# Batch tiles of 256, 256, 512, 512 and 512 rows with sums of four double steps, paired transposes, field sums on VectorE and paced gathers

## The reference

```python
e = jnp.stack([tbl_f[ids[:, f]] for f in range(32)], axis=1)        # (2048, 32, 64)
z = jnp.sum(e, axis=-1)                                             # field sums, 32 columns
outer = jnp.einsum('bpd,pde,bpe->bp', e[:, II, :], kernels, e[:, JJ, :])   # 496 pairs
h = jnp.concatenate([z, outer, dense_ctx], axis=1)                  # 32 + 496 + 16 = 544
h = jnp.maximum(h @ W_top1 + b_top1, 0.0)                           # 512
h = jnp.maximum(h @ W_top2 + b_top2, 0.0)                           # 256
y = h @ W_top3                                                      # 1
```

## Time and profile before

| | |
|---|---|
| median of three executions | 942.61 us |
| time of the profiled execution | 942.61 us |
| its span | 940.8 us |
| PE busy, matmul instructions | 889.5 us (95%), 4592 |
| DVE busy, instructions | 588.2 us (63%), 500 |
| ACT busy, instructions | 139.7 us (15%), 209 |
| POOL busy, instructions | 484.0 us (51%), 518 |
| mean granted TensorE clock | 0.996 of full speed |

### The profile page before, as it was taken

How to read it: one execution, slowest core, us unless ns; L and a number is a source line. 1 busy time by engine, 2 the same in 40 slices (tenths; PEclk the granted TensorE clock), 3 DMA queues, 4 the chain that set the end, 5 groups by cost and what they waited for, 6 DMA issues and landing times.

```text
span 940.8 us, 11425 instructions
## 1 busy us (share of the span) xinstructions
PE 889.5 (95%) x4592; PEld 280.6 (30%) x4592; DVE 588.2 (63%) x500; ACT 139.7 (15%) x209; POOL 484.0 (51%) x518
## 2 busy tenths in 40 slices
PE   0389999999999999999999999999999999999997
PEld 0122222332333323232333333323333333222232
DVE  0146777777655577767764477767775457777850
ACT  0020202012122020020020311002021212002001
POOL 6777777777777777777775346656630000000000
PEclk9989999999999999999999999999999999999999
DMA  9411111111211111121111001111100000000000
GB/s 334 148 26 27 28 27 27 27 27 27 47 28 27 27 27 27 27 47 27 27 27 21 15 14 23 24 38 23 23 16 1 1 0 1 1 2 20 1 1 0
DMA packets 21018, 29.60 MB, mean 31 GB/s; under 512 B 9188, under 2 KB 9316, under 8 KB 20840
## 3 DMA queue, kind: packets, MB, share of 16 engines
q0 software_dynamic: 16384, 16.81, 9.2%
q1 hardware_dynamic: 4576, 12.07, 3.5%
q10 hardware_dynamic: 8, 0.01, 0.0%
HBM read 27.79 MB, written 1.06 MB: 31 GB/s over the span
## 4 chain that ended last, share of the span: by engine, by line
PE 73%; POOL 19%; issue 6%; DMA 1%; ACT 0%; DVE 0%; DVEq 0%; ACTq 0%
PE y L505 39%; PE acc L519 20%; POOL rows L282 19%; PE y L548 6%; PE y L563 3%; PE spin L491 3%; PE spin L530 1%; PE y L553 1%; PE y L572 1%; DMA rows<-tbl,ids_sb 0%; DMA ids_sb<-ids 0%; ACT h L388 0%; DVE prod L462 0%; DVEq L198 0%; ACT h L400 0%
## 5 line engine op out<-in xcount | busy, mean ns | idle before, releaser
L462 DVE TENSOR_TENSOR prod<-y,xt 128x1024 f32<-128x1024 f32 x496 | 587.6, 1220 | 319.5 <-PE y L505 319.5
L282 POOL DMA_INDIRECT rows<-tbl,ids_sb x512 | 483.3, 944 | 210.4 <-issue 151.2
L505 PE MATMUL y<-xt,kw 64*128 64x512 f32 x1984 | 506.5, 624 | 4.7 <-ACT xt L337 4.7
L519 PE MATMUL acc<-prod,ones_strip 128*32 128x512 f32 x1984 | 265.9, 608 | 0.6 <-DVE prod L462 0.6
L505 PEld LDWEIGHTS y<-xt,kw 64*128 64x128 f32 x1984 | 170.1, 187 | 300.7 <-issue 294.0
L337 ACT COPY xt<-spin 128x512 f32<-128x512 f32 x64 | 37.5, 585 | 500.2 <-PE spin L491 500.2
L519 PEld LDWEIGHTS acc<-prod,ones_strip 128*32 128x32 f32 x1984 | 39.1, 108 | 190.2 <-issue 166.0
L491 PE MATMUL spin<-ident,rows 128*128 128x128 f32 x256 | 43.8, 296 | 40.4 <-DMA rows<-tbl,ids_sb 40.4
L548 PE MATMUL y<-h_in,w_sb 128*128 128x512 f32 x128 | 57.1, 599 | 0.7 <-ACT h_in L366 0.7
L491 PEld LDWEIGHTS spin<-ident,rows 128*128 128x128 f32 x256 | 28.0, 145 | 91.4 <-issue 63.9
L548 PEld LDWEIGHTS y<-h_in,w_sb 128*128 128x128 f32 x128 | 23.7, 190 | 34.2 <-issue 32.6
(11 more groups left out here) (19 smaller groups left out, 41.8 us busy)
## 6 DMA issues: line engine op xcount, KB each, us to landing
rows<-tbl,ids_sb POOLq DMA_INDIRECT x512, 2.4
kw<-pair_k SPq DMA_DIRECT2D x14, 512.0 KB, 11.4
w_sb<-w SPq DMA_DIRECT2D x1, 1024.0 KB, 12.8
sums<-z_sums SPq DMA_DIRECT2D x4, 256.0 KB, 2.5
w_sb<-w SPq DMA_DIRECT2D x1, 512.0 KB, 13.7
z_in<-sums SPq DMA_DIRECT2D x8, 64.0 KB
kw<-pair_k SPq DMA_DIRECT2D x1, 384.0 KB, 17.7
ids_sb<-ids SPq DMA_DIRECT2D x1, 256.0 KB, 2.8
```

What stands on the lines that cost most here:

```text
L282: pool.indirect_dma_start(out=rows[:, s, c, h, :], out_offset=None, in_=tables[f], in_offset=bass.IndirectOffsetOnAxis(ap=ids_sb[:, t, c * ...
L462: nc.vector.tensor_tensor(prod[:, n % PROD_SLOTS, :, :], y_banks[u % Y_SLOTS][:, :, :], x, ALU.mult).then_inc(y_read, 1)
L505: last = nc.tensor.matmul(y[:, h, :], kw[part, d, :], xt[part, slot_of(t, units[h][0] // 2), :], start=True, stop=True)
L519: last = nc.tensor.matmul(acc[32 * q:32 * q + 32, :], ones_strip[:, 30 - 2 * s:62 - 2 * s], prod[:, (N_STEPS * t + u // 2) % PROD_SLOTS, u ...
```

## The change

The tiles have 256, 256, 512, 512 and 512 rows now. A group has four double steps (`GROUP = 4`), and there are eight buffers of `prod`. From the second tile on, couples are transposed in pairs, and they go into a `y` buffer instead of `spin`; ACT copies both at once. The bank that is free holds a second `acc`. DVE forms the field sums from the gathered rows, and PE transposes them (two or four transposes for each tile) in place of the 32 sums. The way through DRAM is gone; SP now loads the dense columns into the same rows. POOL's gathers of the first tile have a memset of 128x256 ahead of each, and every later gather waits for a number of finished products, 32 steps ahead of the transpose and one gather for each step (one for every two steps in a narrow tile).

```diff
-TILES = BATCH // TILE
+WIDTHS = [256, 256, 512, 512, 512]
+TILES = len(WIDTHS)
-GROUP = 2
+GROUP = 4
...
-    for j in range(AHEAD):
-        work[N_STEPS - 5 * (AHEAD - j)].append(("transpose", 1, j))
+    work[N_STEPS - GROUP * (AHEAD // 2 + 1)].append(("fields", 0, 0))
+    for j in range(0, AHEAD, 2):
+        work[N_STEPS - GROUP * (AHEAD - j) // 2].append(("couples", 1, j))
...
-    for j in range(COUPLES):
+    for j in range(0, COUPLES, 2):
         n = COUPLES * t + AHEAD + j
         if n < COUPLES * TILES:
-            work[j * N_STEPS // COUPLES + 2].append(("transpose", *divmod(n, COUPLES)))
+            work[j * N_STEPS // COUPLES // GROUP * GROUP + GROUP].append(("couples", *divmod(n, COUPLES)))
     for d, what in zip(MLP_STEPS, (("mlp1", t - 1, 0), ("mlp1", t - 1, 1), ("mlp2", t - 1, 0), ("mlp3", t - 1, 0))):
-        work[d + GROUP].append(what)
+        work[d].append(what)
...
+    work[56].append(("fields", t, 0))
...
+GATHER_LEAD = 32
+def steps_before_gather(t, k, i):
+    what = Y_ORDER[copy_use(t, k)]
+    count = 2 * rowsets(t)
+    return STEPS_BEFORE[what] - GATHER_LEAD + (i + count * (k - what[2])) * 2 * TILE // P // count
...
-                        pool.wait_ge(spin_full, spin_use("transpose", *divmod(n - GATHER_SLOTS, COUPLES)) + 1)
+                        pool.wait_ge(y_full, copy_use(*divmod(n - GATHER_SLOTS, COUPLES)) + 1)
+                        pool.wait_ge(fields_summed, n - GATHER_SLOTS + 1)
                     for h in range(2):
-                        for c in range(ROWSETS):
+                        for c in range(rowsets(t)):
+                            if t > 0:
+                                pool.wait_ge(y_read, steps_before_gather(t, k, rowsets(t) * h + c))
+                            else:
+                                pauses = 2 * rowsets(t) * k + rowsets(t) * h + c
+                                if pauses > 0:
+                                    pool.wait_ge(paused, pauses)
+                                pool.memset(spare[:], 0.0).then_inc(paused, 1)
...
+            def field_sums(t, k):
+                n = couple(t, k)
+                dve.wait_ge(gathered[n % GATHER_SLOTS], rows_in(n))
+                nc.vector.reduce_sum(z_rows[:, 0:rowsets(t), 0, 2 * k:2 * k + 2],
+                                     rows[:, n % GATHER_SLOTS, 0:rowsets(t), :, :], axis=mybir.AxisListType.X
+                                     ).then_inc(fields_summed, 1)
...
-                pe.wait_ge(gathered[s], COUPLE_IN * (n // GATHER_SLOTS + 1))
-                dst = take_spin(spin_use("transpose", t, k))
+                for h in range(count):
+                    pe.wait_ge(gathered[s], rows_in(n))
+                    if h == 0:
+                        y = take_y(copy_use(t, k))
```

More of the change, by code:

```diff
@@ L61 @@
 PAIRS = FIELDS * (FIELDS - 1) // 2
-assert N_STEPS % GROUP == 0 and 4 * UNITS // 2 >= PAIRS and sum(K_CHUNKS) == N_STEPS
+assert sum(WIDTHS) == BATCH and N_STEPS % GROUP == 0 and 4 * UNITS // 2 >= PAIRS and sum(K_CHUNKS) == N_STEPS
 def step_at(*step):
@@ L157, with copy_use, act_uses_through, copied @@
 PLAN = [what for t in range(TILES) for what in plan(t)]
[L159 to L169, removed]
+Y_ORDER = [what for what in PLAN if what[0] not in ("sum", "extra")]
+Y_USES = {what: u for u, what in enumerate(Y_ORDER)}
 def y_use(*what):
     return Y_USES[what]
-def mlp_uses_through(u):
-    return sum(what[0] != "step" for what in Y_ORDER[:u + 1])
+def copy_use(t, k):
+    for what in (("couple", t, k), ("couples", t, k), ("couples", t, k - 1)):
+        if what in Y_USES:
+            return Y_USES[what]
+def act_uses_through(u):
+    return sum(what[0] != "step" for what in Y_ORDER[:u + 1])
+def copied(t, k):
+    return act_uses_through(copy_use(t, k))
+GATHER_LEAD = 32
+STEPS_BEFORE = {}
+_steps = 0
+for _what in PLAN:
+    STEPS_BEFORE[_what] = _steps
+    _steps += _what[0] == "step"
+def steps_before_gather(t, k, i):
+    what = Y_ORDER[copy_use(t, k)]
+    count = 2 * rowsets(t)
+    return STEPS_BEFORE[what] - GATHER_LEAD + (i + count * (k - what[2])) * 2 * TILE // P // count
 def slot_of(t, k):
@@ L256, in couple, with rows_in @@
             return COUPLES * t + k
-        def copied(t, k):
-            return spin_use("transpose", t, k) + 1
-        COUPLE_IN = ROWSETS * 2 * 16
+        def rows_in(n):
+            return sum(16 * 2 * rowsets(m // COUPLES) for m in range(n % GATHER_SLOTS, n + 1, GATHER_SLOTS))
         @block.gpsimd
@@ L448, in _ @@
                 u = y_use("step", t, d)
+                w = WIDTHS[t]
                 dve.wait_ge(y_full, u + 1)
@@ L577, in _ @@
             for what, t, n in PLAN:
-                if what == "transpose":
-                    transpose_couple(t, n)
+                if what == "couple":
+                    transpose_couples(t, n, 1)
+                elif what == "couples":
+                    transpose_couples(t, n, 2)
                 elif what == "step":
```

237 lines of the change are left out of this document (124 added, 113 removed).

## The result

The changed kernel takes 920.7 us, median of four executions (919.28 to 921.07); beside it the kernel before took 942.62 us (942.41 to 942.69). The ratio is 0.9765, with an interval of 0.9748 to 0.9782. The forecast was 919. The profiled execution took 920.92 us, with a span of 918.8.

What follows compares the result with a forecast made beforehand. POOL's gathers pace the first tile, then PE limits. Summed: 294 us to the last gather wait, 185.4, 203.4 and 199.3 for tiles, 34.9 for the end, 917.0 of span, plus 1.8: 919 us, range 904 to 935.

Steps and rivals of the forecast that it cites:

- Four steps to a group: PE in wide tiles: 12 passes and one pair of changes, 5.49 us where two old groups took 5.83.
- the cover of 0.3 us at the fourth step: Wide group: first product frees its `y` buffer at 2.4 us, the fourth step begins at about 2.7.
- A wide tile: PE's time for a 512-row tile: 219.66 less 10.5 (groups), 2.8 (paired transposes), 2.95 (field sums), 203.4 us.
- Narrow tiles: PE in 256-row tiles: passes of 0.215 us, so 2.92 us for a group, 0.73 for each step.
- a sign of being wrong: Listed observations that would refute the forecast, among them PE waiting for DVE inside a group.
- the rival of narrow steps: Narrow passes of 0.265 us, 0.6 us more for each group: 937 us; chance 0.09 shared with DVE at 941.
- The memset: POOL, first tile: about 0.31 us ahead of each of 64 gathers, period 1.56 us, gathers ending at 103.6 us.
- memset free: Rival: the memset fits into POOL's 0.30 us gap, first tile's gathers end at 84 us: 910 us, chance 0.15.
- The chain to the last wait: POOL's gathers and PE's work up to PE transposing couples 8 and 9 of the third tile, at 294 us.
- 53 us of waits: PE between 27.6 and 294 us: some 213 us of work, about 53 us waiting for gathers.
- The clock: PE behind its waits for gathers: a lower clock could cost 3.5 us; none taken, 3.5 kept for the range.
- Gathers behind reductions: Rival: DVE's reductions each hold a gather off by 0.6 us before 294 us: 943 us, chance 0.02.

Runs made afterwards that it cites:

- the second trace of the changed kernel: The changed kernel run once more with no edit, on the chip where the kernel before took 942.52 us: 919.64 us, ratio 0.9759.
- the quick chip: Chip of one follow-up series, where the kernel before took 942.52 us, as in the first timing; the unedited changed kernel took 919.64 us there.
- a late one: Chip where the kernel before took 1118 us; the changed kernel without memsets took 1096.47 us there, without memsets and waits for products 1323.9 us.

## Why the prediction was right

The time came out by two sizes that were off in opposite directions, and in that it was partly luck. The last wait, and all that lies behind it, came as forecast.

- *Four steps to a group*: forecast 5.49 us, measured 5.49. In wide tiles the cover of 0.3 us at the fourth step held.
- *A wide tile*: forecast 203.4 us, measured 203.54. A pair of transposes takes 1.02 us (1.03 forecast), the four transposes of the field sums 0.59 (0.6), by the chain in order of time:

```profile
551.38 1.02 PE y L544 x8
...
588.16 0.59 PE y L587 x4
```

  ACT's copy of a pair was taken at 1.0 us and takes 1.012; DVE's reduction was taken at 0.6 and takes 0.676. These are groups of the changed kernel, by form, as the earlier trace rows:

```profile
L361 ACT COPY xt<-y 128x1024 f32<-128x1024 f32 x24 | 24.3, 1012 | 268.2 <-PE y L544 268.2
L482 DVE TENSOR_REDUCE z_rows<-rows 128x8 f32<-128x512 f32 x48 | 30.8, 676 | 12.7 <-DMA rows<-tbl,ids_sb 12.7
L509 DVE TENSOR_TENSOR prod<-y,xt 128x512 f32<-128x512 f32 x248 | 156.5, 684 | 71.1 <-PE y L559 71.0
L315 POOL MEMSET spare<- 128x256 f32 x64 | 21.0, 328 | 2.0 <-DMA ids_sb<-ids 2.0
```

- *Narrow tiles*: the group was mis-sized, 2.92 us for 3.22. The cover at the fourth step, counted for the wide tile only, fails here. The first product starts 0.75 us after the first step (122.74 to 123.49) and lasts 0.69, so the buffer is free at 124.18 us; three steps of 0.43 us would let the fourth begin at 124.03, and its weight load stands at 124.30 behind a gap of 0.39 us. The trace labels this gap "issue", but the semaphore that PE waits for here is raised at 124.19, with the end of that product. That is PE waiting for DVE inside a group, which the prediction named as a sign of being wrong. It is half of what the rival of narrow steps had (0.6 us for each group). 62 groups at 0.3 us are 19 us. Most of that falls into waits for gathers, but not all: from its wait for a gather at 46.88 us to product 90 at 113.92 PE doesn't wait for gathers, and gathers 65 to 70 and 72 wait for a product; the same holds from 152.84 us to product 32 of the second tile at 192.12. That is some 19 and 8 groups, or 8 us on the chain, an estimate from these traces; no run takes it apart.
- *The memset* was mis-sized the other way: 0.328 us itself (0.31 taken), but the gather behind it starts 0.17 us later where a gather behind a gather needs 0.30. The period is 1.44 us, not 1.56, and the 64 gathers are done 7.7 us sooner. Then POOL waits 6.56 us for a product and starts the 65th at 102.43 us. The forecast had it at 103.6, by POOL's rate, and the products about 2 us behind. Had narrow groups taken 2.92 us, PE would have been at the products up to 5.7 us sooner, and the time would have been some 912 us, near the rival *memset free* (910), which was half true: of the memset's 0.33 us only 0.19 came on top. The quicker feeder and the slower narrow groups cancelled each other.
- *The chain to the last wait*: 294 us forecast, 295.28 measured, and on the way product 32 of the second tile, forecast at 192.5, ends at 192.12 us, with the 129th gather at 192.92. The rest: 623.0 us forecast, 623.5 measured. Missed is how much PE has to spare on the way. The forecast had 53 us of waits between the first step and 294 us. PE waited 46.2 us for gathers in all, in 11 places, but 24.3 of them lie before the first step, so 21.9 are left, in eight pieces of 0.2 to 5.8 us. Its own work there was sized at 213 us and takes some 244: the narrow groups are 19 of the 31 us, and the lower clock some 8.5 at most, an estimate from the granted 0.92, 0.94, 0.86 and 0.86 in the windows of 25 us that begin at 125, 150, 250 and 275 us (17 us at 1.2 GHz before the last wait). So the slack that hides such errors was less than half of what was counted.
- *The clock*: of the 3.5 us kept for the range, 1.7 came. The four steps behind the last wait took 5.33 us, the same later 3.63 (chain in order of time):

```profile
295.94 5.33 PE y L559 x16
...
312.69 3.63 PE y L559 x16
```

  The granted clock is 0.86 in the windows from 250 to 300 us, where PE waited in pieces of 3 to 6 us. I had argued from longer waits that none of it would reach the chain; in this execution it did, by half. In the second trace of the changed kernel the same four steps, behind a wait of 2.50 us, take 3.70 us from their first start to their last end, against 5.40 here, so there none of the loss reached the chain: it differs from one execution to the next. The Trainium skill ("TensorE: Matmul & The Clock Gate", Part 1) has throttling as the default, and this trace agrees in kind.
- *Gathers behind reductions*: 20 of them start in each 25 us of the windows above, 1.25 us apart, beside DVE's reductions. The lock of that rival shows nowhere.

By the runs, of the 22.9 us gained on the quick chip the narrow tiles are 8.3, though by another way than an earlier end of the gathers. The other 14.6 belong to the rest of the change together (groups of four, pairs, field sums on DVE, memsets and waits); no run on that chip takes them apart. What the waits for products cost on a quick chip was not run, so the 896 us worked out for neither memsets nor waits stays untested there. An estimate: with 64 memsets and 143 gathers behind them at full rate, the 208th would start at 3.95 + 64 x 1.44 + 143 x 1.25 = 274.9 us; it starts at 292.7, so they hold it up by at most 17.8 us. With four wide tiles the same sum, with 128 memsets, gives 287.0, and the gather starts at 287.13, so nothing but POOL's own rate (memsets included) holds it there.

## What to carry to other kernels

Find the last moment at which the slow feeder is waited for, and count when it comes and how much work stands behind it. A price paid by the feeder before it counts almost in full (0.19 us x 144 gathers gave 24.5 us of 27), and what the feeder loses behind it is free. What the fed engine loses before it is free only where the feeder doesn't wait for it in turn: of 19 us lost in the narrow groups some 8 counted, by the estimate above, since gathers waited for products. When a forecast hits, check the terms all the same: here two were off, and their errors cancelled. And time in more than one place before a wait that looks useless is taken out: by the estimate the waits for products cost at most 18 us on the quick chip, and on a late one they saved 227.

## What the hardware showed that was not expected

- An indirect gather takes POOL 0.94 us and the next one starts 0.30 us later, 1.25 us from start to start; behind a memset it starts after 0.17 us. A plain transfer of the same 32 KB behind the same memset comes each 0.78 us (its trace has starts at 4.72, 5.50 and 6.28 us).
- In two of the three series, each on its own chip, the kernel before ran 19% and 22% slower, with waits of the other engines that no recorded event ends, while gathers were being issued; behind the last gather a group takes the same 2.91 us as in the first timing, and POOL's gathers stay 1.25 us apart.
